# The first part also runs one batch of the second pair's first attention, and two orders are searched anew

## The reference

```python
x = _layernorm(x + _L0_attn_ref(x, ...))   # 16 heads of 64, plain softmax attention, Wo, bo
x = _layernorm(x + _L0_ffn_ref(x, ...))    # a router picks one of 64 tiles per token, a spline, LayerNorm
x = _layernorm(x + _L1_attn_ref(x, ...))   # linear attention and a 65-wide window attention, gated
x = _layernorm(x + _L1_ffn_ref(x, ...))    # causal attention (16 heads, l2-normed q and k), then 8 experts, soft gate
```

## Time and profile before

| | us |
|---|---|
| median of 3 runs | 2400.33 (2399.95 to 2401.05) |
| profiled execution | 2394.53 |
| its span | 2392.8 |
| part one (start to first xh) | 207.7 |
| part two | 285.7 |
| last xh to the end | 177.5 |
| TensorE busy | 2207.2 (92%) |
| VectorE busy | 1557.9 (65%) |
| ScalarE busy | 1348.8 (56%) |
| GpSimd busy | 848.4 (35%) |

### The profile page before, as it was taken

How to read it: one execution, slowest core, us unless ns; L and a number is a source line. 1 busy time by engine, 2 the same in 40 slices (tenths; PEclk the granted TensorE clock), 3 DMA queues, 4 the chain that set the end, 5 groups by cost and what they waited for, 6 DMA issues and landing times.

```text
span 2392.8 us, 44064 instructions
## 1 busy us (share of the span) xinstructions
PE 2207.2 (92%) x16144; PEld 1537.0 (64%) x16144; DVE 1557.9 (65%) x4247; ACT 1348.8 (56%) x3784; POOL 848.4 (35%) x1010
## 2 busy tenths in 40 slices
PE   8659999999999999999999999999999999998897
PEld 5446666756668566676667666676666856667465
DVE  5567676676657766577755868558676676656642
ACT  5336564764647655476545657366564764546442
POOL 3214561054510643116521346114551064510630
PEclk9879999999999999999999999999999999999899
DMA  4000001000010000110001100100001000010001
GB/s 148 27 1 2 1 2 45 10 32 1 1 53 4 29 1 1 54 33 1 1 10 45 32 1 1 36 19 32 1 1 45 10 32 1 1 45 2 31 1 49
DMA packets 24721, 50.44 MB, mean 21 GB/s; under 512 B 3316, under 2 KB 3900, under 8 KB 24252
## 3 DMA queue, kind: packets, MB, share of 16 engines
q1 hardware_dynamic: 24508, 47.63, 6.2%
HBM read 45.52 MB, written 2.10 MB: 20 GB/s over the span
## 4 chain that ended last, share of the span: by engine, by line
PE 77%; DVE 12%; ACT 5%; POOL 4%; issue 2%; DMA 0%; SPq 0%; DVEq 0%; ACTq 0%
PE ps L1472 10%; PE ps L1493 10%; PE ps L651 5%; PE ps L668 5%; PE ps L602 4%; PE ps L850 4%; PE ps L1410 4%; PE ps L888 4%; PE ps L1505 4%; PE ps L1427 4%; PE ps L781 3%; PE ps L764 3%; PE ps L1365 3%; PE ps L817 2%; PE ps L1376 2%; POOL rn L1715 2%
## 5 line engine op out<-in xcount | busy, mean ns | idle before, releaser
L1030 POOL TENSOR_TENSOR rstd<-ve,half_neg 128x4 f32<-128x4 f32 (+1 forms) x56 | 66.9, 1195 | 979.5 <-DVE ve L1011 979.5
L1493 PEld LDWEIGHTS ps<-wbuf,QK 128*128 128x128 f32 x2048 | 266.0, 191 | 108.2 <-issue 99.9
L1286 POOL TENSOR_TENSOR E<-E,ri 128x512 f32<-128x512 f32 x240 | 247.8, 1041 | 179.7 <-DVE ri L1085 179.1
L1596 ACT ACTIVATE QK<-ps,cols 128x512 f32<-128x512 f32 x256 | 172.9, 687 | 210.1 <-PE ps L1472 209.8
L1472 PE MATMUL ps<-h2T,wbuf 128*128 128x512 f32 x512 | 276.9, 630 | 0.2
L1722 POOL TENSOR_TENSOR work<-work,ri 128x128 f32<-128x128 f32 x480 | 231.8, 508 | 120.8 <-DVE ri L1645 120.0
L1493 PE MATMUL ps<-wbuf,QK 128*128 128x128 f32 x2048 | 270.2, 275 | 0.0
L911 ACT ACTIVATE E<-ps,nm 128x256 f32<-128x256 f32 x480 | 225.5, 484 | 64.3 <-DVE nm L1078 64.0
L1556 ACT ACTIVATE work<-ps,nm 128x128 f32<-128x128 f32 x480 | 198.5, 425 | 99.4 <-DVE nm L1636 99.4
L1715 POOL TENSOR_TENSOR rn<-ss,half_neg 128x8 f32<-128x8 f32 x120 | 195.3, 1638 | 160.1 <-DVE ss L1621 159.3
L1078 DVE TENSOR_REDUCE nm<-ps 128x2 f32<-128x512 f32 x256 | 168.8, 684 | 23.4 <-PE ps L651 21.7
(11 more groups left out here) (280 smaller groups left out, 4490.8 us busy)
## 6 DMA issues: line engine op xcount, KB each, us to landing
wbuf<-in_w SPq DMA_DIRECT2D x128, 256.0 KB, 3.2
xT<-in_xT SPq DMA_DIRECT2D x8, 256.0 KB, 3.5
xr<-in_xr SPq DMA_DIRECT2D x8, 256.0 KB, 4.2
bias_t<-in_bias_t SPq DMA_DIRECT2D x1, 2048.0 KB
out_y<-xn SPq DMA_DIRECT2D x8, 256.0 KB, 2.1
wqkv<-in_wqkv SPq DMA_DIRECT2D x1, 1536.0 KB
wo<-in_wo SPq DMA_DIRECT2D x2, 512.0 KB, 8.2
rows<-in_rows SPq DMA_DIRECT2D x1, 531.0 KB, 7.1
```

What stands on the lines that cost most here:

```text
L1286: nc.gpsimd.tensor_tensor(L.E[:, g % 4, :, :], L.E[:, g % 4, :, :], L.ri[:, g, :].unsqueeze(2).broadcast_to((P, NT, S)), ALU.mult)\
L1493: last = nc.tensor.matmul(bank2[2 + x % 2][:, t * P:(t + 1) * P], hid[:, x % 2, c, t * P:(t + 1) * P], w2[:, x % WB, c, :], start=(c == 0) ...
```

## The change

Part one gets a longer second program. After pair 0's batch 1 (`n` = 0), the same lane `first_b` runs a first attention of pair 1's batch 0 (`n` = 1) from the newly loaded xT. Its output doesn't go to y1 but is copied into `acc`, the experts' accumulator, which is not in use in part one; part two begins with adding it to xb. Part two's first half then runs only batch 1 of pair 1, whose projections were done ahead in part one. The load of the third pair's xT waits for those. Part two becomes a kind of its own, with its own orders. The parts three to eight keep their programs but have other order strings; the last part is unchanged.

```diff
-KINDS = ["first", "both", "both", "last"]
+KINDS = ["first", "second_part", "both", "both", "last"]
...
     ("first", "gpsimd"):
-        "000001011100010101011101100110101000000000",
+        "1110111001010101010100110001100000111111010111011000011110",
+    ("second_part", "gpsimd"):
+        "01111111100111111001111011101110011111111000101011001011111111110110000000110",
     ("both", "gpsimd"):
-        "000111010111100001100110011110101010111111111111101010101010011100010101010101011001000000110",
+        "000111010111100001011010111001110001111111111111100110011011000010111001100110011001000000110",
...
             sp.wait_ge(s["xb_ready"], upto("xb_ready", 1))
-            sp.wait_ge(s["proj1"], upto("proj1", 12))
+            if next_pair == 2:
+                sp.wait_ge(s["pre_proj"], upto("pre_proj"))
+            else:
+                sp.wait_ge(s["proj1"], upto("proj1", 12))
...
                     if u == 0 and n:
-                        pe.wait_ge(s["y1_ready"], upto("y1_ready", n))
+                        pe.wait_ge(s["y1_ready"], upto("y1_ready", n if L.tag == "1" else NP))
+                        if L.tag == "2":
+                            pe.wait_ge(s["x_next"], upto("x_next", 32))
...
+        def early_pe(pe):
+            yield from first_heads_pe(pe, first_b, 1, 0, 0)
+            yield from first_heads_pe(pe, first_b, 0, 1, 1)
+
+        def first_pe(pe, p):
+            both = p > 0
             if both:
-                yield from first_heads_pe(pe, first_a, 0, 0, None)
-                yield from first_heads_pe(pe, first_a, 1, 1, 0)
+                if p == 1:
+                    yield from first_heads_pe(pe, first_a, 1, 0, None)
+                else:
+                    yield from first_heads_pe(pe, first_a, 0, 0, None)
+                    yield from first_heads_pe(pe, first_a, 1, 1, 0)
...
             dve.wait_ge(sem_of(L, "wo_done"), upto("wo_done" + L.tag, n + 1))
+            if L.tag == "2" and n:
+                nc.vector.tensor_copy(acc[:, 0:NT, :], tri(L.bank[0][:, 0:S], 2)).then_inc(s["early_ready"], 1)
+                return
...
+                if p == 1:
+                    yield
+                    dve.wait_ge(s["xb_ready"], upto("xb_ready", 1))
+                    nc.vector.tensor_tensor(y1[:, 0:NT, :], acc[:, 0:NT, :], xb[:, 0:NT, :], ALU.add)\
+                        .then_inc(s["y1_ready"], 1)
+                    yield from first_heads_dve(dve, first_a, 1, 0, None)
...
                     if p:
                         pe.wait_ge(s["out_used"], upto("out_used", NE + 1))
                     else:
-                        pe.wait_ge(s["y1_ready"], upto("y1_ready", NP))
+                        pe.wait_ge(s["early_ready"], upto("early_ready", 1))
                 if u >= 3:
                     pe.wait_ge(s["pre_copied"], upto("pre_copied", u - 2))
-                first_proj(pe, bank2[u % 3], 0, u).then_inc(s["pre_proj"], 1)
+                first_proj(pe, bank2[u % 3], 0 if p else 1, u).then_inc(s["pre_proj"], 1)
```

More of the change, by code:

```diff
@@ L69 @@
-    ("both", "vector"):
[L70 to L74, removed]
+        "1110111001010101010100110001100000111111010111011000011110",
@@ L87 @@
     ("both", "sync"):
-        "1111101111",
+        "1111110111",
     ("last", "vector"):
@@ L436, in whole_net @@
         COUNT.update(dict.fromkeys("""
+            exp2
+        """.split(), (64, 64, 64, 64, 32)))
+        COUNT.update(dict.fromkeys("""
             dve1
-        """.split(), (61, 61, 61, 0)))
+        """.split(), (61, 61, 61, 61, 0)))
         COUNT.update(dict.fromkeys("""
-            exp1 exp2
-        """.split(), (32, 64, 64, 32)))
+            exp1
+        """.split(), (32, 32, 64, 64, 32)))
+        COUNT.update(dict.fromkeys("""
+            ri2 norm2 w_trn2
+        """.split(), (32, 32, 32, 32, 16)))
@@ L921, in first_heads_act, with early_act, first_act @@
                             .then_inc(sem_of(L, "et_act"), 1)
-        def first_act(act, both):
-            if both:
-                yield from first_heads_act(act, first_a, 0, 0, None)
-                yield from first_heads_act(act, first_a, 1, 1, 0)
+        def early_act(act):
+            yield from first_heads_act(act, first_b, 1, 0, 0)
+            yield from first_heads_act(act, first_b, 0, 1, 1)
+        def first_act(act, p):
+            both = p > 0
+            if both:
+                if p == 1:
+                    yield from first_heads_act(act, first_a, 1, 0, None)
+                else:
+                    yield from first_heads_act(act, first_a, 0, 0, None)
+                    yield from first_heads_act(act, first_a, 1, 1, 0)
             else:
@@ L1103, in first_heads_dve, with early_dve, first_dve @@
                 .then_inc(s["y1_ready"], 1)
-        def first_dve(dve, both):
+        def early_dve(dve):
+            yield from first_heads_dve(dve, first_b, 1, 0, 0)
+            yield from first_heads_dve(dve, first_b, 0, 1, 1)
+        def first_dve(dve, p):
+            both = p > 0
             link = Chain(dve, "dve1")
             if both:
-                yield from first_heads_dve(dve, first_a, 0, 0, None)
-                yield from first_heads_dve(dve, first_a, 1, 1, 0)
+                if p == 1:
+                    yield
[3 more added lines that the diff above has]
+                    yield from first_heads_dve(dve, first_a, 1, 0, None)
+                else:
+                    yield from first_heads_dve(dve, first_a, 0, 0, None)
+                    yield from first_heads_dve(dve, first_a, 1, 1, 0)
                 dve.wait_ge(s["y1_ready"], upto("y1_ready", NP))
@@ L1288, in first_heads_pool, with early_pool, first_pool @@
                     .then_inc(sem_of(L, "norm"), 1)
-        def first_pool(pool, both):
+        def early_pool(pool):
+            yield from first_heads_pool(pool, first_b, 1, 0)
+            yield from first_heads_pool(pool, first_b, 0, 1)
+        def first_pool(pool, p):
+            both = p > 0
             yield
@@ L1296, in first_pool @@
             if both:
-                yield from first_heads_pool(pool, first_a, 0, 0)
-                yield from first_heads_pool(pool, first_a, 1, 1)
+                if p == 1:
+                    yield from first_heads_pool(pool, first_a, 1, 0)
+                else:
+                    yield from first_heads_pool(pool, first_a, 0, 0)
+                    yield from first_heads_pool(pool, first_a, 1, 1)
             else:
```

162 lines of the change are left out of this document (97 added, 65 removed).

## The result

The changed kernel takes 2409.44 us (median of 5 runs, 2406.71 to 2412.35) against 2400.11 for the kernel before: ratio 1.0041, 95% interval 1.0030 to 1.0052. It is slower by 0.4%, where I had forecast a gain of 11 us.

What follows compares the result with a forecast made beforehand. TensorE throughput bounds part two and middle parts; part one has a hole at its serial VectorE router chain. +18 (part one) − 26 (part two) − 3 (later parts) = −11 us, from 2400.3 to 2389; likeliest 2380 to 2395, full range 2366 to 2406.

Steps and rivals of the forecast that it cites:

- Part two shrinks by 26: Part two, relieved of one batch's first attention and projections: −26 us, to 260; bounds −38 and −15.
- winning 3: Part two behind the second attentions: two chain steps move ahead of the experts, saving 3 us.
- The stage before the scores: Part two's second attentions, V products to first scores: 21 us instead of 25.2 and 24.9, saving 8 us.
- The score steps: Part two's second attentions: a loop of 4.5 us per score step instead of 4.76 and 5.38, saving 8 us.
- The tails: Part two, last scores to the next start: about 12.5 us alone instead of 16.3, saving 7 us over both.
- Part one grows by 18: Part one, which receives the early batch: +18 us, from 207.7 to about 226; bounds +5 and +38.
- the collisions: Part one's router chain: GpSimd normalisations delaying VectorE's SBUF products, 1 us; as a rival 12.5 us, no change, chance 0.14.
- given back 8: Part one's router chain: clock 1.00 instead of 0.50 makes the chain's own products lose 8 us.
- The rival that the chain waits behind the early batch: Part one's chain advances at the attention's pace, growth from 29 us on, priced at +38; total 2409 us; chance 0.16.
- the free ride of +5: Part one's hole takes the batch nearly free, +5; with part two's −38, 2364 us; full or mixed chance 0.22.
- The other parts −3: The six later parts, same instructions in new orders: −0.5 us each, −3 in all.
- signs of being wrong: Part one growing under 10 or over 28 us, part two's scores staying 5 apart, later parts moving over 1 each.

Runs made afterwards that it cites:

- experiment 7: Experiment 1's kernel (changed kernel, old orders in parts three to eight) with other searched orders for parts one and two: 2395.43 us, ratio 0.9985 to the kernel before.
- experiment 1: Changed kernel with parts three to eight put back on their old orders: 2403.11 us, ratio 1.0021 to the kernel before.
- experiment 3: Changed kernel with part two's one remaining first attention left out on all four engines: 2410.12 us, part two 280.5 us.
- Experiment 4: Experiment 3's kernel with the missing attention's matmuls and transposes put back, unread and without waits: 2413.95 us, part two 276.1 us.
- experiment 2: Kernel before with the changed kernel's new middle-part orders, run in parts two to eight: 2404.30 us, ratio 1.0023.
- experiment 6: Changed kernel with 20 instead of 6 idle matmuls behind part two's second attention: 2413.87 us, ratio 1.0058 to the kernel before.

## Why the prediction was wrong

The stages of the two second attentions, in us, by the starts of V products (L1365 then, L1445 now), first scores, eighth scores, and the copy to acc; the first column is part three of before, the others part two; experiment 7 is the first of the two kernels above:

| | before | forecast | after | no first attention | its matmuls alone | experiment 7 |
|---|---|---|---|---|---|---|
| V to first scores | 25.2 | 21 | 26.0 | 24.5 | 24.5 | 24.4 |
| seven score steps | 33.3 | 31.5 | 33.4 | 33.9 | 33.1 | 33.1 |
| tail, to next V | 16.3 | 12.5 | 13.9 | 17.2 | 13.9 | 13.5 |
| V to first scores | 24.9 | 21 | 23.8 | 24.3 | 23.7 | 24.2 |
| seven score steps | 37.7 | 31.5 | 34.1 | 33.8 | 33.5 | 33.2 |
| tail, to acc copy | 17.4 | 13.9 | 15.7 | 15.2 | 15.6 | 14.3 |
| xh to second acc copy | 156.3 | 133 | 148.4 | 150.3 | 145.8 | 144.4 |
| TensorE busy, clock | 149.3, 1.00 | | 126.2, 0.94 | 109.5, 0.82 | 125.5, 0.94 | 122.5, 0.96 |

**Part two shrinks by 26: the step that failed.** It gave 4 us. The second attentions gave 7.9 instead of 23, and the rest behind them cost 2.9 (133.4 for 130.5) instead of winning 3. Another 1.1 is that part two of before was already that much shorter than its part three, on which the steps are read. The 2.9 go with the clock, 0.94 there: with the same instructions the rest takes 130.2 us at 0.97 in experiment 1, where the win is then 0 and not 3. I named the right mechanism, the second attention's own pace, and mis-sized every term of it.
- The stage before the scores: −8 forecast, −0.3 measured. I had counted the V products, GpSimd's 8 powers and 4 us for the ends, 3.7 + 13.3 + 4 = 21 us. Experiments 3 and 4 show that it takes 24.5 with the first attention's work on the other engines gone. GpSimd's first and last powers in experiment 3, whose V products start at 224.87 and first scores at 249.38:

```profile
231.07 4.89 POOL L1800 TENSOR_TENSOR rn<-ss,half_neg 128x8 f32<-128x8 f32 x3 [9.65 <-DVE ss L1706]
...
242.12 3.24 POOL L1800 TENSOR_TENSOR rn<-ss,half_neg 128x8 f32<-128x8 f32 x2 [0.30 <-DVE ss L1706]
```

That makes 6.2 us to the first power, 14.3 for the eight with their gaps and 4.0 behind them. In part three of before the same pieces are 6.2, 15.7 and 3.4, so an unbroken row of powers had some 2 us to give and not 4. In the chain of after only three of GpSimd's powers stand there, 4.9 us together; from 239 to 246 us it runs through VectorE steps of 0.6 us one behind the other.
- The score steps: −8 forecast, −3.5 measured. The loop of 4.5 us is there, to a hundredth: in experiment 3 the scores from the fourth on start 4.51 us apart, in six of eight steps to the hundredth. But there the first three steps take 5.1 to 5.5 us, with score matmuls of 1.61 us at half clock in place of 0.88. In after three steps of the first attention are of that kind (4.9 to 5.2 us), and the last step of the second takes 6.4 us (351.82 to 358.22): the first attention's output projection, 3.57 us of TensorE (L937, from 353.15), stands ahead of the eighth scores.
- The tails: −7 forecast, −4.1 measured.

Behind all three stands what I left out: taking TensorE work away lowered the granted clock of what remained, to 0.94 in after and 0.82 in experiment 3, from 1.00. I counted the clock as a gain in part one and not as a loss in part two. Experiment 4 against 3 puts it at 4.5 us where the whole first attention goes; in the changed kernel itself, at clock 0.94, no run prices it alone, but the same orders took 1.6 us less in the second attentions and 3.1 less behind them in experiment 1, where the clock was higher behind them (0.97 for 0.94).

**Part one grows by 18: right in size, +17.8** (13 to 18 over the executions), but by errors inside it that offset each other. The router chain grew by 10.6 (76.2 us from y1 at 95.10 to the window scores, against 65.55) for 11, the window stretch by 5.1 for 7, and 2.1 lie before them, where I had none: y1 comes at 95.10 instead of 93.04. Inside the chain the collisions cost 4.2 instead of 1; 3.2 of these go with the normalisations, the rest with an addition on GpSimd. The clock, at 0.84 over the chain and not 1.00, can hardly have given back 8. So what I counted from the strings as late, 18 us, was too much: chain growth less collisions leaves 6.4 for late steps less the clock's gain, where I had 10. No run separates these two. The rival that the chain waits behind the early batch, from +29 on, did not happen, and neither did the free ride of +5. That rival's total, 2409, is the time measured, by luck: part one grew by less than 29 and part two gave 4, not 26.

**The other parts −3: wrong.** The new orders cost 5 us by themselves (experiment 2) and 4.8 to 6.3 in the changed kernel (experiment 1). I had found no stretch that they could lengthen by much. In part four of after the first score steps come 0.6 us later than in part three of before, the second copy to acc 0.2, the transposes of the window steps begin 0.9 later and the next xh 1.9. Part of it is again the clock. The windows from 156 to 186 us behind xh, in parts four and six of after and part three of before, read:

```profile
951.38:981.38 30.00, 26.82 (x114) 16.34 (x115) 15.87 (x58) 15.19 (x21) 2.28 (x2) 0.83 0.06 17
1527.76:1557.76 30.00, 26.50 (x122) 16.53 (x123) 17.13 (x61) 15.88 (x22) 2.29 (x2) 0.89 0.06 18
649.44:679.44 30.00, 26.75 (x124) 16.87 (x125) 18.35 (x68) 15.88 (x22) 2.29 (x2) 0.89 0.06 18
```

Parts four and seven of after have 0.83 there and take 288.7 us; parts five and six, with the same orders, have 0.89 and take 287.7 and 287.3. Before has 0.89 in parts three to seven, at 286.7 to 286.8. So some 1 to 1.4 us of a long part go with the lower clock and 0.6 to 0.9 remain without it. Which digits carry either I can't say.

**The sum.** Of +9.3 us by medians 4.8 to 6.3 are the later parts' orders. What remains without them, +3.9 in experiment 1 (2403.11 against 2399.23), is part one's growth less what part two returns. The forecast's sign hung on part two returning more than part one takes. Experiment 7 shows that this is possible, but only just: its medians lie 3.8 us under the kernel before. In its profiled execution it is +12.3 and −11.0, against the short one of before. Two of my own signs of being wrong came: the later parts moved by over 1 us each, and the score steps of part two still took 4.8 and 4.9 us on average, not 4.5.

## What to carry to other kernels

Before moving work out of a full stretch, ask what its length becomes when only the other work is left: take the serial chain's pace from the chain's own pieces, all of them, and check it by leaving the work out, once with its matmuls and once without. Count TensorE's clock on both sides, where work arrives and where it leaves. When a change comes with new orders for parts that it doesn't touch, price those apart: here they were at least half of the loss.

## What the hardware showed that I had not expected

- Matmuls that nobody reads made a stretch faster: 280.5 us for part two without the first attention, 276.1 with its matmuls alone, as the clock from xh to the second acc copy went from 0.82 to 0.94. Those are single executions, and the totals don't show it. Idle matmuls ahead of a stretch of waits (experiment 6) gained nothing. The Trainium skill, "TensorE: Matmul & The Clock Gate", section "Part 1: The HAM clock gate (the "warmup" mystery)", names two levels, 1.2 and 2.4 GHz, of which activity selects one; the trace agrees, with 1.61 against 0.88 us for the same eight score matmuls.
- Identical instructions in identical orders took 281.75 and 277.1 us in part two of two kernels that differ only later, through where the clock fell. Differences of under 5 us in one part need more than one profile.
- A VectorE product of 0.22 us takes up to 1.19 us beside GpSimd, five times as long; one of 0.69 us (L1193 of before) took 1.97, less than three times.
